# Row attention of a four-stage block: small products in strips of the TensorE array, and two vector steps moved to GpSimd

## The reference, cut to what matters

```python
s_n = _layernorm(s, ln_s_w, ln_s_b)
pair_bias = einsum('bqkc,ch->bhqk', _layernorm(z), w_z)
q, k, v = (einsum('bsqc,cx->bsqx', s_n, w).reshape(B, S, R, 8, 32) for w in (w_q, w_k, w_v))
logits = einsum('bsqhd,bskhd->bshqk', q / sqrt(32), k) + mask_bias + pair_bias
attn = softmax(logits, axis=-1)
o = einsum('bshqk,bskhd->bsqhd', attn, v).reshape(B, S, R, 256)
g = sigmoid(einsum('bsqc,cx->bsqx', s_n, w_g) + b_g)
out = einsum('bsqx,xc->bsqc', o * g, w_o) + b_o
x = x + out
```

## Time and profile before

| | us |
|---|---|
| median of 3 runs (2251.46 to 2258.72) | 2254.99 |
| profiled execution, span | 2253.2 |
| TensorE matmul busy, whole span | 1661.3 (74%) |
| VectorE busy | 1572.7 (70%) |
| ScalarE busy | 842.9 (37%) |
| GpSimd busy | 586.2 (26%) |

### The profile page before, as it was taken

How to read it: one execution, slowest core, us unless ns; L and a number is a source line. 1 busy time by engine, 2 the same in 40 slices (tenths; PEclk the granted TensorE clock), 3 DMA queues, 4 the chain that set the end, 5 groups by cost and what they waited for, 6 DMA issues and landing times. The chain is left out here.

```text
span 2253.2 us, 32914 instructions
## 1 busy us (share of the span) xinstructions
PE 1661.3 (74%) x9803; PEld 1264.7 (56%) x9803; DVE 1572.7 (70%) x3607; ACT 842.9 (37%) x2302; POOL 586.2 (26%) x476
## 2 busy tenths in 40 slices
PE   0006005999999998378878788739999588769997
PEld 0006004788878887356767666516667444646665
DVE  7999966777777775376888876664455334667777
ACT  3211003767766774110434331323443222333432
POOL 0555002223223320074777776000000000300000
PEclk9999999999999996588888888869999799589999
DMA  8000000000000000310000011000000721000000
GB/s 298 0 2 2 0 0 13 0 0 0 0 0 0 0 0 1 14 9 5 9 8 8 8 8 8 16 5 12 7 19 19 178 58 28 19 1 19 19 19 19
DMA packets 71692, 46.74 MB, mean 21 GB/s; under 512 B 23969, under 2 KB 66770, under 8 KB 71122
## 3 DMA queue, kind: packets, MB, share of 16 engines
q1 hardware_dynamic: 59634, 41.78, 7.3%
q0 software_dynamic: 9984, 3.21, 1.9%
q10 hardware_dynamic: 2016, 1.06, 0.2%
HBM read 32.44 MB, written 13.45 MB: 20 GB/s over the span
## 5 line engine op out<-in xcount | busy, mean ns | idle before, releaser
L1867 DVE SCALAR_TENSOR_TENSOR sb_X<-x_py,sb_x_gc,sb_X 128x128 f32 (+1 forms) x768 | 269.2, 351 | 187.4 <-PE x_py L1807 161.1
L1127 POOL DMA_INDIRECT sb_ge_gs<-source_rows,sb_ge_idx x288 | 289.9, 1007 | 127.9 <-issue 85.9
L1796 PE MATMUL x_pu<-sb_TT,sb_x_w 128*128 (+1 forms) x512 | 248.4, 610 | 78.2 <-PEq L1822 76.2
L1807 PEld LDWEIGHTS x_py<-sb_x_w,sb_x_ht 128*128 128x128 f32 x2048 | 248.1, 192 | 60.8 <-issue 39.5
L1786 ACT ACTIVATE sb_x_ht<-x_pu,sb_x_b 128x512 f32<-128x512 f32 x256 | 174.4, 687 | 252.8 <-PE x_pu L1796 252.6
L1807 PE MATMUL x_py<-sb_x_w,sb_x_ht 128*128 128x128 f32 x2048 | 249.6, 275 | 1.3 <-DVE sb_X L1867 1.3
L1499 PE MATMUL acc<-sb_ge_b,sb_ge_ol 128*128 128x320 f32 x576 | 202.6, 490 | 56.4 <-DVE sb_ge_b L1286 56.4
L238 POOL TENSOR_TENSOR sb_bias<-sb_PB,sb_TT 128x1024 f32<-128x1024 f32 x64 | 150.7, 2355 | 338.4 <-DVE sb_logits L265 338.4
L322 ACT ACTIVATE sb_probs<-sb_logits,sb_neg_max 128x128 f32<-128x128 f32 x512 | 198.4, 390 | 6.7 <-DVE sb_neg_max L276 3.3
L1796 PEld LDWEIGHTS x_pu<-sb_TT,sb_x_w 128*128 128x128 f32 x512 | 88.6, 193 | 170.9 <-issue 85.5
L1499 PEld LDWEIGHTS acc<-sb_ge_b,sb_ge_ol 128*128 128x128 f32 x576 | 113.3, 213 | 96.8 <-DVE sb_ge_b L1286 62.5
(11 more groups left out here) (402 smaller groups left out, 3318.3 us busy)
## 6 DMA issues: line engine op xcount, KB each, us to landing
sb_ge_gs<-source_rows,sb_ge_idx POOLq DMA_INDIRECT x288, 2.4
sb_z<-in_L_conv_z SPq DMA_DIRECT2D x1, 4096.0 KB, 20.4
sb_TT<-in_L_conv_mask SPq DMA_DIRECT2D x1, 4096.0 KB, 42.8
x_rows<-sb_X SPq DMA_DIRECT2D x4, 1024.0 KB, 5.1
normed_rows<-sb_TT SPq DMA_DIRECT2D x4, 1024.0 KB, 6.2
sb_X<-x_rows SPq DMA_DIRECT2D x2, 2048.0 KB, 22.4
sb_mr_xg<-normed_rows SPq DMA_DIRECT2D x32, 128.0 KB, 2.6
out<-sb_X SPq DMA_DIRECT2D x8, 512.0 KB, 5.3
```

What stands on the lines that cost most here:

```text
L1127: pool.indirect_dma_start(GS[:, j, k, :], None, SRC_T, bass.IndirectOffsetOnAxis(ap=IDX[:, j, k:k + 1], axis=0))\
L1796: nc.tensor.matmul(PU[c % 2][:, :], w1[:, c * P:(c + 1) * P], TT[:, ds(g * BANK, BANK)], start=True, stop=True)\
L1807: last = nc.tensor.matmul(bank[:, (e % 4) * C:(e % 4 + 1) * C], HT[:, u, e * chunks + c, k * P:(k + 1) * P], w2[:, e * chunks + c, :], sta ...
L1867: last = nc.vector.scalar_tensor_tensor(out=xs, in0=PY[(k * YB + b) % NY][:, (e % 4) * C:(e % 4 + 1) * C], scalar=GC[:, u, k * experts + e ...
```

## The change

- Scores: Q and K are copied out of PSUM by one VectorE copy of 512 columns into `QK`; no block-diagonal `KT` is built. Each head's scores are a product of its own: 32 rows deep, 128 by 128, operands on partitions 32r to 32r+31, output in PSUM bank r. Heads are stored in an order in which consecutive products use strips r = 0, 1, 2, 3.
- Values: `V` is the weight block (128x32) and the turned probabilities are the moving operand (128 columns), so the output is already turned: 32 partitions by 128 columns, at partitions 32r. The two transposes of L422 go. V is scaled by 0.5 when it is copied.
- Row-sum factors: the inverse sum of each head, repeated over 32 columns, is the weight block of a product with the identity (128 columns); its output stands at the partitions of the turned values. VectorE then forms gate times factor (`GN`) and turned values times `GN` (`OGT`).
- Output bias and input norm: both on GpSimd, as an add of a broadcast `b_o` to the residual tile and a `tensor_scalar`. The product of depth one is gone.
- Turned probabilities go to the upper halves of the four score banks; ScalarE copies them from there. Q, K and V are made a turn earlier (the loop has 14 rounds of 4 turns), buffers of logits, maxima, V and gate are deepened.
- `pair_bias` writes its heads in the new order. GpSimd's list is unrolled.

New order of a turn s. TensorE: scores s+1; Q and K of s+2; output product s-1; transposes of s (after the exponentials of s and the logits of s+1); values and gate of s+2; input transpose of s+3; factors and values of s. VectorE: `GN` and `OGT` of s-1 with the statistics of s-2 between; logits s+1; residual s-1; maximum s+1; Q and K copy of s+2; inverse sums of s; scale and shift of s+3. ScalarE: eight exponentials of s; two copies of s; V and two tanh of s+2.

The diff, cut to its core (lines of the kernel after):

```diff
@@ pair_bias
-                bias = PB[:, :, n * half:(n + 1) * half]
+                shape = [P, HEADS // 2, 2, half]
+                bias = PB[:, :, n * half:(n + 1) * half].rearrange("p (r j) k -> p r j k", j=2)
...
@@ row_attention, buffers
-        L = bank("p_logits", (P, 2, BANK))
-        TA, TB = bank("p_turned_a"), bank("p_turned_b")
-        QPS, PRV, TURN, O = bank("p_q"), bank("p_vg"), bank("p_xn"), bank("p_out")
+        L = bank("p_logits", (P, QUAD, BANK))
+        QKP, VG, XO, RO = bank("p_qk"), bank("p_vg"), bank("p_xn_out"), bank("p_sum_heads")
+        scored = lambda h: (h % QUAD) * 2 + h // QUAD
+        turned_of = lambda h: L[:, h // 2, HALF + (h % 2) * T:HALF + (h % 2 + 1) * T]
...
@@ sync
-                             (bo[:, :], A["b_o"].unsqueeze(0))):
+                             (bo[:, :], A["b_o"].partition_broadcast(P))):
@@ gpsimd, for each tile: norm(s + 3), bias(s + 2), out_bias(s + 3)
+            def norm(s):
+                if s >= 2:
+                    pool.wait_ge(xn_turned, s - 1)
+                nc.gpsimd.tensor_scalar(XN[:, s % 2, :], X2[:, s * C:(s + 1) * C], mean[:, s:s + 1], rstd[:, s:s + 1],
+                                        ALU.subtract, ALU.mult).then_inc(xn_made, 1)
+            def out_bias(s):
+                pool.wait_ge(xn_made, s + 1)
+                xs = X2[:, s * C:(s + 1) * C]
+                nc.gpsimd.tensor_tensor(xs, xs, bo[:, :], ALU.add).then_inc(xbo_made, 1)
@@ vector, turn(s), in its new order
+                if real(s - 1):
+                    after(v, pv_done, s)
+                    nc.vector.scalar_tensor_tensor(out=GN[:, :, :], in0=TH[:, (b - 1) % KEPT, :, :], scalar=1.0,
+                                                   in1=RO[:, 0:HALF].rearrange("p (a q) -> p a q", a=2), op0=ALU.add, op1=ALU.mult).then_inc(gate_made, 1)
...
+                    nc.vector.tensor_tensor(OGT[:, :, :], RO[:, HALF:].rearrange("p (a q) -> p a q", a=2), GN[:, :, :], ALU.mult).then_inc(ogt_made, 1)
+                if real(s + 1):
+                    after(v, score_done, s + 2)
+                    after(v, bias_made, s + 2)
+                    after(v, exp_b, s)
...
+                if real(s + 2):
+                    after(v, qk_done, s + 3)
+                    after(v, score_done, s + 2)
+                    nc.vector.tensor_copy(QK[:, :, :, :].rearrange("p w j k -> p (w j k)"), QKP[:, :]).then_inc(qk_out, 1)
...
@@ scalar, turn(s): eight exponentials of tile s, two copies of tile s, then
+                    after(act, vg_done, s + 3)
+                    after(act, ogt_made, s - 1)
+                    nc.scalar.activation(V[:, (b + 2) % KEPT, :], VG[:, 0:HD], ACT.Copy, scale=0.5)
...
@@ tensor, turn(s), in its new order
+                if real(s + 1):
+                    after(pe, qk_out, s + 2)
+                    after(pe, logit_made, s + 1)
+                    after(pe, tb_out, s)
                     for j in range(2):
+                        for r in range(QUAD):
+                            strip = slice(r * DH, (r + 1) * DH)
+                            last = nc.tensor.matmul(L[:, r, j * T:(j + 1) * T], QK[strip, 0, j, :], QK[strip, 1, j, :],
+                                                    start=True, stop=True)
...
+                if real(s):
+                    after(pe, inv_made, s + 1)
+                    after(pe, ogt_made, s)
+                    for j in range(2):
+                        for r in range(QUAD):
+                            h = j * QUAD + r
+                            nc.tensor.matmul(RO[r * DH:(r + 1) * DH, j * T:(j + 1) * T], RI[:, h:h + 1].to_broadcast([T, DH]),
+                                             ident[:, :], start=True, stop=True)
+                    after(pe, vg_out, s + 1)
+                    for j, turned_out in enumerate((ta_out, tb_out)):
+                        after(pe, turned_out, s + 1)
+                        for r in range(QUAD):
+                            h = j * QUAD + r
+                            last = nc.tensor.matmul(RO[r * DH:(r + 1) * DH, HALF + j * T:HALF + (j + 1) * T],
+                                                    V[:, b % KEPT, h * DH:(h + 1) * DH], PT[:, h, :], start=True, stop=True)
```

More of the change, by code:

```diff
@@ L207, in row_attention @@
         block = ctx.enter_context(nc.Block())
         X2 = X[:, :, :].rearrange("p s c -> p (s c)")
-        carried = sem("att_carried")
         N_W = 10
         real = lambda s: not isinstance(s, int) or 0 <= s < F
+        upto = lambda s: min(s, F) if isinstance(s, int) else s
+        scored = lambda h: (h % QUAD) * 2 + h // QUAD
+        turned_of = lambda h: L[:, h // 2, HALF + (h % 2) * T:HALF + (h % 2 + 1) * T]
         def turns(engine, turn):
-            for s in (-2, -1, 0, 1):
-                turn(s, s % 2)
-            with engine.Fori(0, (F - 4) // 4) as i:
+            first, last = 5, F - 3
+            for s in range(-3, first):
+                turn(s, s)
+            with engine.Fori(0, (last - first) // 4) as i:
@@ L218, in turns @@
                 for u in range(4):
-                    turn(i * 4 + (2 + u), u % 2)
-            for s in (F - 2, F - 1, F, F + 1):
-                turn(s, s % 2)
+                    turn(i * 4 + (first + u), first + u)
+            for s in range(last, F + 2):
+                turn(s, s)
         @block.sync
@@ L249, in _ @@
+            norm(0)
+            norm(1)
+            bias(0)
+            norm(2)
+            bias(1)
+            pool.wait_ge(w_in, 16 * N_W)
+            for s in range(3):
+                out_bias(s)
+            for s in range(F - 2):
+                if s + 3 < F:
+                    norm(s + 3)
+                bias(s + 2)
+                if s + 3 < F:
+                    out_bias(s + 3)
         @block.vector
         def _(v):
-            nc.vector.memset(ones[:, :], 1.0).then_inc(ones_set, 1)
@@ new lines, in turn @@
+                    last.then_inc(out_done, 1)
+                if real(s):
+                    after(pe, exp_a, s + 1)
+                    after(pe, logit_made, upto(s + 2))
+                    for h in range(4):
+                        last = nc.tensor.transpose(turned_of(h), PR[:, b % 2, h, :], ident[:, :])
+                    last.then_inc(ta_done, 1)
+                    after(pe, exp_b, s + 1)
+                    for h in range(4, 8):
+                        last = nc.tensor.transpose(turned_of(h), PR[:, b % 2, h, :], ident[:, :])
+                    last.then_inc(tb_done, 1)
@@ L412, in turn @@
+                if real(s + 2):
+                    after(pe, vg_out, s + 2)
+                    nc.tensor.matmul(VG[:, 0:HD], SNT[:, :], wv[:, :], start=True, stop=True)
+                    for a in range(2):
+                        last = nc.tensor.matmul(VG[:, HD + a * T:HD + (a + 1) * T], wg[:, a * P:(a + 1) * P], SNT[:, :],
                                                 start=True, stop=True)
                     last.then_inc(vg_done, 1)
[L414 to L418 removed]
@@ L419, in turn @@
-                if real(s - 1):
-                    after(pe, og_made, s)
-                    for a in range(2):
-                        last = nc.tensor.transpose(TA[:, a * T:(a + 1) * T], OG[:, a * P:(a + 1) * P], ident[:, :])
-                    last.then_inc(og_turned, 1)
+                if real(s + 3):
+                    after(pe, xn_made, s + 4)
+                    after(pe, x_added, s)
+                    after(pe, sn_made, s + 3)
+                    nc.tensor.transpose(XO[:, 0:T], XN[:, (b + 3) % 2, :], ident[:, :]).then_inc(xn_turned, 1)
```

230 lines of the change are left out of this document (79 added, 151 removed).

## The result

| | before | after |
|---|---|---|
| median, us | 2253.22 (2249.66 to 2258.72, 4 runs) | 2109.78 (2108.68 to 2110.78, 4 runs) |
| profiled execution, span, us | 2253.2 | 2108.7 |
| a turn of the attention stage, us | 7.74 | 5.58 |

The account below looks back on a forecast made before the run. TensorE was taken to bound the attention stage. Turns falling from 7.74 to 6.1 us save 103 us over 63, plus 5 at the ends: 2253.2-108 = 2145 us profiled, 2147 median; range 2120 to 2205.

Parts of the forecast that it names:

- The changes of shape: TensorE's entries into another strip shape: three in a new turn at 0.20 us each, 0.60 us.
- TensorE's list: All TensorE work in a new attention turn, from scores to values and shape changes: 5.27 us.
- rival 3: TensorE's holes make the clock fall: 2390 us with all the stage at 1.2 GHz, half about 2265; chance 0.04.
- rival 1: TensorE's strips overlap only in part, a set takes about 0.9 us: 2200 us; chance 0.13.
- rival 2: Column strips take turns, factors and values cost 1.79 us each: 2285 us, with row strips too 2367; chance 0.09.
- The new ring: ScalarE's chain from exponentials through transposes, V and gate products to V and tanh sets the turn: 6.02 us.
- the jump: The attention loop's jump, taken from the old turn and added to each new one: 0.11 us.
- V and gate products: TensorE's products behind the last transposes, for which V and tanh wait: 0.97 us.
- V and two tanh: ScalarE's last steps in its ring, V's copy and two tanh: 1.05 us.
- the ends: Both ends of the attention stage, where the last tile's path loses the same products: 5 us saved (0 to 10).
- The second ring: From values through `GN`, `OGT`, logits, transposes, V and gate back to factors and values: 5.6 us, not setting the turn.
- The bias product 0.48: TensorE's bias product with the switch back, removed by the change: 0.48 us a turn.

Follow-up runs that it names:

- e12: The changed kernel with both order moves of e3 and the attention turns written out instead of looped: 2085.66 us, ratio 0.9249.
- e8: The changed kernel with row-sum factors and values given 128 columns of weights, so no products overlap (three heads of four wrong): 2285.05 us, ratio 1.0142.
- e2: The changed kernel with TensorE's V and gate products ahead of the transposes of the probabilities: 2107.89 us, ratio 0.9359.
- e3: The changed kernel with V and gate products ahead of the transposes and VectorE's inverse sums ahead of the Q and K copy: 2089.15 us.
- e9: The kernel before, with four gate buffers so that tanh waits for the product of two turns earlier: 2254.70 us, ratio 0.9995.
- e10: The kernel before, with all attention turns written out, without the hardware loop: 2246.80 us, ratio 0.9964.
- e11: The changed kernel with all attention turns written out, without the hardware loop: 2111.02 us, ratio 0.9362.
- e5: The changed kernel with the output bias back as a product of depth one on TensorE, GpSimd's output bias gone: 2132.63 us, ratio 0.9466.
- e4: The changed kernel with loop order exchanged in scores and factors, so consecutive products use the same strip twice: 2112.14 us, ratio 0.9375.

## Why the prediction was wrong where it was

**What held.** Sixteen passes in four strips cost what four cost, 0.46 us forecast and 0.46 measured, for column strips too, which stood in no row. The changes of shape were forecast at three times 0.20 us. In e12, where TensorE never waits, they are 0.48 in all: its timeline has the factors at 559.92, the values at 560.38, the scores at 560.93, Q and K at 561.59, the output product at 562.58, the input transpose at 564.90 and the next factors at 565.11. So from values to scores it takes 0.55 us instead of the 0.46 of a set, the scores 0.66, the eight passes of Q and K 0.99 instead of 0.90, and the input transpose 0.21 instead of 0.11. Into and out of row strips the price is 0.19 to 0.20, half of it ahead of the first pass and half behind it; from the whole array into column strips it is 0.10. TensorE no longer sets the turn, as forecast, and ScalarE waits before V (0.28 us ahead of L350). TensorE's list was forecast at 5.27 us and is 5.17 in e12 over all turns, 5.19 in most; the changes and the V product are shorter than laid out, the eight transposes 0.13 longer (0.99). The clock stayed at 1.00, so rival 3 fell; rival 1 with a set of 0.9 us fell with the first row; rival 2 didn't come, and e8 shows that it would have cost what it was given. The Trainium skill (TensorE: Matmul & The Clock Gate, Part 3) states 2.38 times for three column strips. For four, e8 against after gives 1.89/0.46 = 4.1, and 3.9 against the 0.112 us a pass of the earlier trace rows: more for each strip than the page has. The same page's figure of some 62 ns a matmul ("Wait — 56ns, not 53.3ns?"), given for decoding by microcode, is not what bounds here: 0.46/16 is 29 ns a pass, and even a whole product of two passes takes 58.

**What failed** is the step "The new ring", sized at 6.02 us plus 0.11 for the jump. The ring was the right one: ScalarE waits in it where forecast, and e2 and e3 show that it holds the turn together with a second one. Its terms were too long. The trace of after has 5.59:

| term | forecast | measured |
|---|---|---|
| exponentials | 3.10 | 3.10 |
| last sum, hop, weight load, transposes | 0.69 | 0.63 |
| V and gate products | 0.97 | 0.88 |
| tail and hop | 0.21 | 0.20 |
| V and two tanh | 1.05 | 0.78 |
| jump | 0.11 | 0 |

The largest is V and two tanh. I took V's length from one start to the next, 0.43 us, although its own record in the earlier trace rows is 0.37; e9 shows that 0.17 of it was a wait. And I took the tanh pair's record of 0.62 to its end, while the next exponential starts 0.50 us after the first tanh (569.86-569.36). With V to tanh at 0.28 that is 0.78. The jump's 0.11 was about right for the old kernel (0.14 by e10) and wrong to add to a ring through ScalarE while TensorE has holes (e11). V's product was taken at 0.52 us, the distance from its start to the next in the earlier trace rows; in after that distance is 568.43-568.00 = 0.43. The single records of before have 0.30 us from L409's first pass to its second and 0.22 from there to L411; why the first is longer there is not shown. In all 0.54 us a turn too much. Against the 6.1 that went into the sum, 0.52 x 63 = 33 us, and 3 more at the ends (8 against 5): 2147-36 = 2111, and 2109.8 was measured.

**The second ring** was laid at 5.6 us. A ring of that length there is (5.56 in e2), but on another path, so that the number is luck. I closed it through the logits, the transposes and the V and gate products. In after, L391 does follow the logits, but TensorE then waits at L415 for VectorE, so that path has slack. The trace closes the ring through the output product, the residual, the maximum, the Q and K copy and the inverse sums, all in VectorE's order. So "with 0.4 us to spare" was false: there was none, and had the first ring been still shorter, the second would have held the turn (e2). I had summed VectorE's work, 4.7 us (4.6 measured), and left it at that, without walking from the first instruction that waits for TensorE to the last for which TensorE waits.

**The range** failed by its low end, 2120. "A turn of 5.8 to 6.4" allowed 0.3 us under the sum, though V, tanh and the V product were all taken at an upper end: records with their tails, starts with the waits between them. A term read as a start-to-start distance in a trace where the engine is not the bound is an upper bound, and I had put it in as a value.

**GpSimd.** Rightly hidden; the norm took 0.80 us instead of the 0.57 of the row of its size. "The bias product 0.48" was counted among TensorE's savings, and e5 shows that it was worth 0.40 a turn, though by the chain through the residual and not by TensorE's load.

## What to carry to other kernels

In this kernel small products in different 32-row or 32-column strips ran wholly beside each other (0.46 us for sixteen passes instead of 1.89), and each change of shape cost one to two passes of the whole array (0.10 to 0.20 us); put them into few, large sets. When an engine stops being the bound, lay out every closed chain through the lists of all engines, not only the one that looks fullest, and take for each step its own record, not the distance to the next start. If a move in one list gives nothing, try it together with the move that relieves the other chain before it is dropped: here 0, 2 and 21 us.

## What was unexpected of the hardware

- Sixteen passes of eight float32 products in four strips run in four groups, one every 0.11 us. Within a group they start 7 ns apart where neighbours in the list use different strips, and 14 to 18 ns where they share one, and in the set behind those; the set takes 0.46 us in both (e4).
- A jump of the hardware loop cost a full TensorE about 0.6 us in the kernel before (0.14 a turn by e10, every fourth turn) and 0.3 in e3 (by e12); with holes it cost nothing that shows (e11).
- GpSimd's `tensor_scalar` of 128x128 with an operand per partition takes 0.80 us, where the row of the same size in the earlier trace rows takes 0.57, and the add of two tiles 0.46.
- The two passes of the bias product, with the change into their shape, delay the result by 0.41 us (e5), while the change out of it took the place of a wait.
- Into and out of row strips a change of shape costs 0.19 to 0.20 us, from the whole array into column strips only 0.10 (e12).
